# Attention and gated feed-forward: near halves of four row blocks loaded first, three late forms cast ahead of decode, decode dealt out from the second period

## The reference

```python
def _L0_xattn_ref(text, features, Wq, bq, Wk, bk):
    Q = jnp.einsum('btx,dx->btd', text, Wq) + bq
    K = jnp.einsum('bpx,dx->bpd', features, Wk) + bk
    scores = jnp.einsum('btd,bpd->btp', Q, K) * scale
    attn = jax.nn.softmax(scores, axis=-1)
    return jnp.einsum('btp,bpd->btd', attn, features)

def dequant_nf4(q, absmax, shape):
    w = NF4_CODE[q.reshape(-1)]
    w = w.reshape(-1, BLOCK) * absmax[:, None]
    return w.reshape(shape)

# feed-forward: HD 1024, M 3584
g = jnp.einsum('bsh,mh->bsm', x, Wg)
u = jnp.einsum('bsh,mh->bsm', x, Wu)
h = jax.nn.silu(g) * u
return jnp.einsum('bsm,hm->bsh', h, Wd)

x = x + _L0_xattn_ref(_layernorm(x), ctx, Wq, bq, Wk, bk)
x = x + _L0_ffn_ref(_layernorm(x), ...)
```

## Time and profile before

| | us |
|---|---|
| median of 3 runs | 1919.1 (1917.35 to 1922.13) |
| the profiled execution | 1918.35 |
| its span, first to last instruction | 1916.2 |
| PE busy in it | 1898.2 |
| DVE / ACT / POOL busy | 1623.0 / 1448.2 / 370.3 |
| preparation, about | 0 to 100 |
| attention, about | 100 to 405 |
| gate and up, the last of the attention between | 364 to 1399 |
| down | to the end |

### The profile page before, as it was taken

One profiled execution on the slowest core, in us unless ns is written; L12 is line 12 of the kernel. 1 busy time (PEld: TensorE's weight loads), 2 busy tenths in 40 slices (PEclk: granted clock), 3 DMA queues, 4 the chain that ended last, 5 costly groups with the idle time before them and its releaser, 6 DMA issues.

```text
span 1916.2 us, 29499 instructions
## 1 busy us (share of the span) xinstructions
PE 1898.2 (99%) x9758; PEld 963.7 (50%) x9758; DVE 1623.0 (85%) x2694; ACT 1448.2 (76%) x2697; POOL 370.3 (19%) x568
## 2 busy tenths in 40 slices
PE   9999999999999999999999999999999999999999
PEld 4487888744444444444444444444444444444444
DVE  7978999869889899899898888898798898896963
ACT  3887776588998988988988988988999999900000
POOL 2023353301111121121121121121123222210110
PEclk9999999999999999999999999999999999999999
DMA  9338999955554565454454454465679988974462
GB/s 356 71 85 189 259 262 276 309 156 130 118 145 125 119 152 130 114 153 130 113 153 126 112 157 120 114 159 134 143 192 225 249 228 217 229 254 131 156 234 84
DMA packets 437640, 326.14 MB, mean 170 GB/s; under 512 B 371680, under 2 KB 371952, under 8 KB 435568
## 3 DMA queue, kind: packets, MB, share of 16 engines
q1 hardware_dynamic: 393280, 170.55, 39.6%
q0 software_dynamic: 44032, 153.65, 25.0%
q10 hardware_dynamic: 176, 0.07, 0.0%
HBM read 154.31 MB, written 82.31 MB: 123 GB/s over the span
## 4 chain that ended last, share of the span: by engine, by line
PE 72%; ACT 12%; DVE 8%; issue 4%; DMA 0%; SPq 0%; DVEq 0%; POOL 0%; ACTq 0%
PE ps L2294 39%; PE ps L2337 23%; PE ps L1682 7%; ACT sq L347 4%; ACT sq L343 3%; PE ps L1650 2%; PE ps L1717 2%; DVE w L363 1%; DVE tail L2447 1%; ACT halves L415 1%; ACT tail L2368 1%; ACT w L347 1%; ACT w L343 1%; ACT tail L2383 1%; DVE halves L431 1%
## 5 line engine op out<-in xcount | busy, mean ns | idle before, releaser
L2294 PE MATMUL ps<-T,wS 128*128 128x512 f16 x4704 | 1017.7, 379 | 5.1 <-DVE ps L2402 2.5
L2294 PEld LDWEIGHTS ps<-T,wS 128*128 128x128 f16 x4704 | 459.6, 98 | 560.0 <-issue 6.7
L347 ACT ACTIVATE sq<-sq 128x512 f32<-128x512 f32 x898 | 516.9, 628 | 0.0
L363 DVE SCALAR_TENSOR_TENSOR w<-sq,w 128x512 f32<-128x512 f32 x590 | 415.9, 705 | 117.0 <-ACT sq L347 107.7
L343 ACT ACTIVATE sq<-q 128x512 f32<-128x512 int32 x598 | 363.9, 632 | 49.1 <-DVE w L363 48.6
L2337 PE MATMUL ps<-T,tail 128*128 128x512 f16 x1584 | 346.7, 380 | 3.9 <-DVE tail L2489 2.7
L2337 PEld LDWEIGHTS ps<-T,tail 128*128 128x128 f16 x1584 | 155.2, 98 | 192.8 <-issue 5.8
L431 DVE SCALAR_TENSOR_TENSOR halves<-w,halves 128x512 f16<-128x512 f32 x240 | 163.0, 688 | 6.4 <-ACT halves L415 6.1
L2337 PE MATMUL ps<-T,wS 128*128 128x512 f16 x768 | 168.4, 379 | 0.0
L2242 POOL DMA_DIRECT2D keep_h<-tail x196 | 106.2, 542 | 292.0 <-DVE tail L2447 291.7
L415 ACT CAST halves<-w 128x512 f16<-128x512 f32 x204 | 126.7, 622 | 43.2 <-DVE w L363 31.6
(11 more groups left out here) (244 smaller groups left out, 1868.6 us busy)
## 6 DMA issues: line engine op xcount, KB each, us to landing
keep_h<-tail POOLq DMA_DIRECT2D x196, 256.0 KB, 2.5
tail<-keep_h POOLq DMA_DIRECT2D x66, 512.0 KB, 4.9
wS<-keep_h POOLq DMA_DIRECT2D x32, 512.0 KB, 4.9
...
```

Of the source, the lines that this page charges most:

```text
L347: nc.scalar.activation(place, place, ACT.Square, bias=b, scale=a).then_inc(un.s_act, 1)
L363: nc.vector.scalar_tensor_tensor(out=out, in0=square_place(un, u, i - 1), scalar=FACTORS[i - 1][1], in1=un.w[:, buf, :], op0=ALU.add, op1= ...
L2294: last = nc.tensor.matmul(ps[:, bank, :], un.wS[:, z % SLOTS, a, kt, :], t.Tp[side][product][:, :, b, kt, :], start=fresh and n == 0, stop ...
```

## The change

There are three parts. First, near halves of four blocks (`NEAR_FIRST`) stand ahead in SP's queue, then the four pairs of far halves, each two pairs with one semaphore; DVE's maxima and POOL's wait follow. Second, at the end of the attention, forms 11, 12 and 13 are cast ahead of decode phase 5 on ACT and DVE; phase 6 has no run of its own any more and is taken in with phase 7. Third, `deal` starts at slot 28 instead of 56, the credit of (9, 14) in the first dealt period becomes (5, 7) in each of the first two, and in slots 14 to 27 DVE may take 3 steps in every second pass.

```diff
--- before.py
+++ after.py
@@ -97,7 +97,7 @@
 GROUP_OUT = (None, (0, 0), (0, 1), (1, 0), (0, 1), (1, 1), (1, 0))
 FRESH_GROUPS, KEPT_GROUPS, ROW_GROUPS, PRE_GROUPS, PART_OF = (0, 2, 3), (2, 3), (1, 4, 5, 6), (4, 5, 6), {4: 2, 6: 3}
 SAVED_IN_W = 2
-CREDIT, FULL, FORMS_END = (9, 14), (35, 50), 9
+CREDIT, CREDIT_OVER, FULL, FORMS_END = (5, 7), 2, (35, 50), 9
 DOWN_STEPS = PRODUCTS * CH_PAIRS
 DOWN_SQ_RING = 6
 ATTEND_PHASES = 10
@@ -625,9 +625,9 @@
 
         period, dealt = 4 * PIECES, {}
         steps = (2 * (4 * STEPS + 4 + PIECES), 2 * (4 * OPS + PIECES))
-        for first in range(2 * period, SLOT_COUNT, period):
+        for first in range(period, SLOT_COUNT, period):
             other = [other_work(k) for k in range(first, first + period)]
-            whole = [steps[e] + sum(o[e] for o in other) + (CREDIT[e] if not dealt else 0) for e in range(2)]
+            whole = [steps[e] + sum(o[e] for o in other) + (CREDIT[e] if first <= CREDIT_OVER * period else 0) for e in range(2)]
             if first + period == SLOT_COUNT:
                 whole = [FULL[e] * period // 10 for e in range(2)]
             given, spent = [0, 0], [0, 0]
@@ -656,7 +656,7 @@
             k = phase - HIDDEN_PHASE
             if k < LATE_SLOTS:
                 return (0, 0, 0, 0, 2, 2, 2, 1, 1, 1, 1)[k], (0, 0, 3, 3, 0, 3, 3, 4, 4, 4, 4)[k]
-            return self.dealt[k] if k in self.dealt else ((2 if k // SPLIT_STEPS % 2 or k % 2 else 3), 6)
+            return self.dealt[k] if k in self.dealt else ((2 if k % 2 else 3), 6)
         return 8, 9 if phase - DOWN_PHASE < FORMS_END else 10
 
 PLAN = Plan()
@@ -836,9 +836,9 @@
     TURNED_TILES = TB
     BIAS_AFTER = 2
     WARM_UP = 15
-    BY_HALVES = 2
+    BY_HALVES, NEAR_FIRST = 2, 4
     BY_POOL = 2
-    WMAX = KT + BY_HALVES + 1
+    WMAX = KT + NEAR_FIRST + 1
     EVICTS_IN = {0: (0, 1, 2, 3)}
     SUMS_IN = {1: (0,), 2: (1, 2), 3: (3,), 4: (4,), 5: (5, 6), 6: (7, 8), 7: (9, 10)}
     SQUARES_IN = {3: (0,), 4: (1,)}
@@ -931,13 +931,15 @@
 
         sp.dma_start(wk(0)[:, 0:BANK], t.Wk[0:P, 0:BANK]).then_inc(s_w[0], 16)
         sp.dma_start(wq(0)[:, P:BANK], t.Wq[0:P, P:BANK]).then_inc(s_bias_in, 16)
-        sp.dma_start(wk(1)[:, 0:BANK], t.Wk[P:2 * P, 0:BANK]).then_inc(s_w[1], 16)
-        sp.dma_start(wq(1)[:, 0:BANK], t.Wq[P:2 * P, 0:BANK]).then_inc(s_w[1], 16)
-        for k in range(BY_HALVES):
+        for k in range(1, NEAR_FIRST):
             rows = slice(k * P, (k + 1) * P)
-            sp.dma_start(wq(k)[:, BANK:DIM], t.Wq[rows, BANK:DIM]).then_inc(s_far[k], 16)
-            sp.dma_start(wk(k)[:, BANK:DIM], t.Wk[rows, BANK:DIM]).then_inc(s_far[k], 16)
-        for k in range(BY_HALVES, KT - 1):
+            sp.dma_start(wk(k)[:, 0:BANK], t.Wk[rows, 0:BANK]).then_inc(s_w[k], 16)
+            sp.dma_start(wq(k)[:, 0:BANK], t.Wq[rows, 0:BANK]).then_inc(s_w[k], 16)
+        for k in range(NEAR_FIRST):
+            rows = slice(k * P, (k + 1) * P)
+            sp.dma_start(wq(k)[:, BANK:DIM], t.Wq[rows, BANK:DIM]).then_inc(s_far[k // 2], 16)
+            sp.dma_start(wk(k)[:, BANK:DIM], t.Wk[rows, BANK:DIM]).then_inc(s_far[k // 2], 16)
+        for k in range(NEAR_FIRST, KT - 1):
             rows = slice(k * P, (k + 1) * P)
             sp.dma_start(wq(k), t.Wq[rows, :]).then_inc(s_w[k], 16)
             sp.dma_start(wk(k), t.Wk[rows, :]).then_inc(s_w[k], 16)
@@ -1042,7 +1044,7 @@
         pool.wait_ge(s_bias_in, 49)
         for k in range(BY_POOL):
             pool.wait_ge(s_w[k], 32)
-            pool.wait_ge(s_far[k], 32)
+            pool.wait_ge(s_far[k // 2], 64)
             for j, row in enumerate((wq(k), wk(k))):
                 nc.gpsimd.tensor_tensor(sums[:, j, :] if k == 0 else pool_tmp[:, j, :], row, bqk[:, 1 - j, k:k + 1].broadcast_to([P, DIM]),
                                         ALU.mult).then_inc(s_made, 1)
@@ -1190,14 +1192,14 @@
             nc.vector.tensor_scalar(t.y_out[:, :], t.y_out[:, :], 1.0 / (H_BOUND_SCALE * W_SCALE), None, ALU.mult)
 
         for side, cols in enumerate((slice(0, BANK), slice(BANK, DIM))):
-            for k in range(BY_HALVES):
-                dve.wait_ge(s_far[k] if side else s_w[k], 32)
+            for k in range(NEAR_FIRST):
+                dve.wait_ge(*((s_far[k // 2], 64) if side else (s_w[k], 32)))
                 if side == 0 and k == 0:
                     dve.wait_ge(s_bias_in, 48)
                 place = KT + k if side else k
                 nc.vector.tensor_reduce(wmax[:, 0, place:place + 1], wq(k)[:, cols], axis=AX.X, op=ALU.max, apply_absolute_value=True)
                 nc.vector.tensor_reduce(wmax[:, 1, place:place + 1], wk(k)[:, cols], axis=AX.X, op=ALU.max, apply_absolute_value=True)
-        for k in range(BY_HALVES, KT):
+        for k in range(NEAR_FIRST, KT):
             dve.wait_ge(s_w[k], 32)
             nc.vector.tensor_reduce(wmax[:, 0, k:k + 1], wq(k), axis=AX.X, op=ALU.max, apply_absolute_value=True)
             if k < KT - 1:
@@ -1875,12 +1877,11 @@
         for i in range(TB):
             y_normalise(nc, act, t, LAST, i)
         then.copied(act, 4)
-        streams.act.run(HIDDEN_PHASE + 5)
         late_hi(nc, act, t, 11)
         late_hi(nc, act, t, 12)
         then.copied(act, 5)
-        streams.act.run(HIDDEN_PHASE + 6)
         late_hi(nc, act, t, 13)
+        streams.act.run(HIDDEN_PHASE + 5)
         for m in range(14, 18):
             late_hi(nc, act, t, m)
             then.copied(act, m - 8)
@@ -2083,11 +2084,10 @@
         then.combined(dve, 4)
         for n in range(4):
             t_sum(dve, nc.vector.tensor_tensor, t, LAST, n)
+            if n < 2:
+                late_lo(nc, dve, t, 11 + n)
+        late_lo(nc, dve, t, 13)
         streams.dve.run(HIDDEN_PHASE + 5)
-        late_lo(nc, dve, t, 11)
-        late_lo(nc, dve, t, 12)
-        streams.dve.run(HIDDEN_PHASE + 6)
-        late_lo(nc, dve, t, 13)
         for m in range(14, 18):
             late_lo(nc, dve, t, m)
             then.combined(dve, m - 8)
```

## The result

| | before | after |
|---|---|---|
| median of 15 runs, us | 1919.1 (1917.24 to 1924.31) | 1922.56 (1921.13 to 1929.8) |
| the profiled execution, us | 1918.35 | 1921.13 |
| its span | 1916.2 | 1919.3 |
| end of PE's last product | 1912.58 | 1914.94 |

The ratio of after to before is 1.0020, with a 95% interval of 1.0011 to 1.0029: 2.1 to 5.6 us slower, less than the 5.8 us that the prediction called a measurable change. The time lies within the predicted range and 2.7 us over the number. But the two traces show that one of the three terms, the largest, had the wrong cause.

A forecast was written before the change was run, and what follows sets the result against it. PE was taken to bound the kernel, busy 1898.2 of 1916.2 us, so only shortening its waits counts. Terms +1.2 + 0.8 - 1.2 = +0.8 us put the profiled execution at 1919.15 and the median at 1919.9, range 1915.3 to 1923.8.

The forecast's parts named there:

- likeliest case: Whole kernel: the forecast itself, terms +1.2, +0.8 and -1.2 us, giving 1919.9 us; chance 0.46.
- the prediction's own signs of being wrong: Block starts don't move, ACT casts form 15 earlier than 0.3 us behind before, or slot 50 waits 2 us or more.
- All that follows lands 1.27 us later: Preparation loads: blocks 2 and 3 take 6.34 us as halves, 5.07 as full rows, delaying later loads; taken as 1.2.
- first rival: Preparation: halves load at the full rate, so part 1 is 0; sum -0.4 us, 1918.7; chance 0.20.
- So 3.9 us are left: Preparation, GpSimd: products end near 26.3, the maximum over partitions is wanted at 29.0 + 1.2, leaving 3.9 us.
- PE's head start: Preparation: PE would start block 0's split products about 0.65 us earlier, but would still wait for DVE at block 2.
- short wait expected near 19.2: Preparation: PE wants block 4 at 19.2, but it lands at 19.8, so a short wait.
- rival that ACT never catches up: Decode: ACT over 5 us behind at pass 35, waits of 7 us instead of 3.2; +5.8 us, 1924.9; chance 0.07.
- All three do what they are for: Whole kernel: all targeted waits go, -1.2 - 1.8 - 3.2 = -6.2 us, 1912.9; chance 0.06.
- the new deal clears every wait: Decode: no wait is left, -3.2 there, -1.2 us in sum, 1917.9; chance 0.17.
- the change does nothing: Decode: steps up to slot 80 are bound by data, not by the deal; 1919.1 us; chance 0.04.
- slower rival: Decode: ACT stays behind and stages 3, 5 and 7 make PE wait; +5.8 us, 1924.9; chance 0.07.

The follow-up runs named there:

- e1_near: The kernel before with part 1 of the change alone (near halves of four row blocks first): 1923.27 us against 1918.21, ratio 1.0024.
- e7_no_credit: The changed kernel with ScalarE's credit in the deal set to 0 instead of 7: 1920.03 us against 1918.54 for the kernel before, ratio 1.0003.

## Why the prediction was right or wrong

**The number**: +0.8 was forecast, the profiled executions differ by +2.8 and the medians by +3.5. The range held it, but not because part 1 was understood: its term came out at +2.4, above its own upper bound of 1.8. The likeliest case had the right sign, and of its terms two are right in cause. By the prediction's own signs of being wrong, one came: the block starts did not move to 24.9. They went from 23.71 to 22.79, which is within what executions of the same loads differ by. The other two did not (form 15 was cast 0.9 us later, and slot 50 waited 0.88 us).

**Part 1, +1.2 forecast, +2.4 in the traces.** Two steps failed, one each way.
- "All that follows lands 1.27 us later" rested on 331 GB/s for half rows, one stretch of one trace. The changed kernel moved 389 and 357 GB/s with half rows; in e1_near, with the same loads, 325 and 367. From 5 to 8 us nine traces with the new loads moved 287 to 389 and five with the old 305 to 331; from 8 to 12 us the new moved 341 to 385 and the old 384 to 401. Over both stretches the means are 361 and 362: no rate was lost. And DVE was done between 27.57 and 28.53 in the nine, on average at 28.05, and between 27.74 and 28.75 in the five, on average at 28.16. Block 6 was reached at 22.79, not at 24.9. The first rival (half rows cost no rate) was right in that, and 1918.7 still was not the time.
- "So 3.9 us are left" for GpSimd is the step that cost the forecast its cause. It took the whole idle time of the earlier trace rows for slack, since its releaser was DVE. Of the 7.80 us, 6.1 to 7.2 are what the switch to the maximum takes in the other traces, which leaves 0.6 to 1.7 us of slack, not 3.9 behind products that are 5 us later. By the prediction's own end of the products, 26.3, plus 6.6, the maximum would have been put at 32.9, and the term near +4; with the measured end it is 31.48. The section of the Trainium skill named above, which gives 6 us, was there to be weighed, and was not.
- Right: PE's wait at 12.27 went, PE's head start brought nothing, and the shift of the scale (2.43 us at the RECIPROCAL) reached 79.29 whole. The short wait expected near 19.2 did not come, since the blocks were not late.

**Part 2, +0.8 forecast, +0.84 measured.** This term is right in cause and size, and the chain was right step by step: waits of 1.4 and 1.6 us before products 8 and 9 were forecast, 1.31 and 1.46 came; the cast of form 15 was put 0.9 us later, and from the L2300 row it stands 7.96 us off for 7.04 before. The wait at product 7 and that at form 13 went.

**Part 3, -1.2 forecast, -0.84 in waits, -1.18 in PE's time.** The places are right: no wait at slot 46, 79 and 107, one at 50 (0.7 forecast, 0.88 came) and one at 78 (1.3 forecast, 1.51 came). The size of each was 0.2 short, and that -1.2 came out as PE's time is luck: the prediction counted waits alone, 3.2 less 2.0, and left out the 0.16 us that each wait costs besides. The rival that ACT never catches up falls; e7_no_credit shows that the credit itself made the wait at slot 50.

**Rivals.** "All three do what they are for" falls with part 2, "the new deal clears every wait" with the waits at slots 50 and 78, and "the change does nothing" with the new wait at slot 50. The slower rival, with its end at 1924.9, placed the danger in the decode; the loss was in the preparation, in a mechanism that no rival named.
